# Twelve saved tiles instead of eight, and a new order of work around group 0, in a conditioned residual block

## The reference

```python
hidden = concatenate([cond, cond], -1)                      # (4, 512)
x_mean = mean(x, axis=1, keepdims=True)                     # (4, 1, 512)
fused  = concatenate([x, x_mean * ones, hidden * ones], -1) # (4, 1024, 1536)
out    = x + relu(einsum('bld,do->blo', fused, W) + b)      # W (1536, 512)
```

## Time and profile before

| | |
|---|---|
| median of 3 runs | 104.46 us |
| the profiled execution's own time | 105.41 us |
| its span, first to last instruction | 103.3 us |
| TensorE busy | 96.9 us (94%) |
| VectorE busy | 80.9 us (78%) |
| ScalarE busy | 47.3 us (46%) |
| GpSimd busy | 41.5 us (40%) |
| TensorE's granted clock | 1.0 of full speed in every slice |
| HBM traffic | 12.91 MB read, 8.39 MB written, 206 GB/s over the span |

### The profile page before, as it was taken

The page is one execution under the profiler, slowest core; times in us unless marked ns, Lnnn a source line. Parts: engine busy times, 40 slices in busy tenths (PEclk is TensorE's granted clock), DMA queues, the critical chain, the costliest instruction groups (busy, mean ns, idle before and its releaser), DMA issues.

```text
span 103.3 us, 1722 instructions
## 1 busy us (share of the span) xinstructions
PE 96.9 (94%) x523; PEld 78.2 (76%) x523; DVE 80.9 (78%) x146; ACT 47.3 (46%) x116; POOL 41.5 (40%) x37
## 2 busy tenths in 40 slices
PE   5959999999999999999999999999999999999940
PEld 2339999778888786888888886888888868888930
DVE  3173578999899999999999966999999976557630
ACT  3267335795508379497396002973951007310000
POOL 1029700000000003999846501488485089992000
PEclk9999999999999999999999999999999999999999
DMA  2999999999999997999999595000780870595994
GB/s 61 293 300 261 234 233 238 268 274 249 268 296 232 251 226 222 254 244 274 303 331 293 154 229 162 0 0 0 181 226 0 210 196 1 171 290 132 251 309 168
DMA packets 35439, 21.39 MB, mean 207 GB/s; under 512 B 2021, under 2 KB 33129, under 8 KB 35433
## 3 DMA queue, kind: packets, MB, share of 16 engines
q1 hardware_dynamic: 33848, 20.13, 78.9%
q10 hardware_dynamic: 1584, 1.18, 4.3%
HBM read 12.91 MB, written 8.39 MB: 206 GB/s over the span
## 4 chain that ended last, share of the span: by engine, by line
PE 89%; ACTq 4%; ACT 2%; issue 0%; DVE 0%
PE ps_y L459 76%; PE ps_y L560 4%; PE ps_y L562 4%; PE ps_y L561 4%; ACTq L168 2%; ACTq L158 2%; PE ps_mean L478 1%; PE ps_const L527 1%; ACT xh L259 1%; ACT w1h L252 1%; ACT L244 0%; DVE w L449 0%; PE ps_y L583 0%; ACT act_warm L244 0%
## 5 line engine op out<-in xcount | busy, mean ns | idle before, releaser
L234 POOL TENSOR_TENSOR xa<-xa,back 128x512 f32 x28 | 36.1, 1314 | 45.1 <-DVE back L346 45.1
L459 PE MATMUL ps_y<-xh,w1h 128*128 (+2 forms) x128 | 43.9, 370 | 1.1 <-ACT w1h L252 1.1
L459 PE MATMUL ps_y<-xl,w1h 128*128 (+2 forms) x128 | 43.0, 363 | 0.0
L459 PE MATMUL ps_y<-xh,w1l 128*128 (+2 forms) x128 | 42.9, 363 | 0.0
L259 ACT ACTIVATE xh<-ps_xt 128x512 fp32r<-128x512 f32 (+1 forms) x36 | 19.8, 550 | 19.4 <-DVE ps_xt L333 19.4
L459 PEld LDWEIGHTS ps_y<-xh,w1h 128*128 128x128 f32 x128 | 22.6, 188 | 6.7 <-ACT xh L259 1.6
L339 DVE TENSOR_TENSOR xl<-ps_xt,xh 128x512 fp32r<-128x512 f32 (+1 forms) x36 | 22.2, 618 | 4.7 <-ACT xh L259 4.7
L333 DVE STREAM_TRANSPOSE ps_xt<-xa 128x512 f32<-128x512 f32 (+1 forms) x36 | 22.3, 642 | 4.5 <-DMA xa<-in_x_dram 4.2
L459 PEld LDWEIGHTS ps_y<-xh,w1l 128*128 128x128 f32 x128 | 22.6, 189 | 3.8
L459 PEld LDWEIGHTS ps_y<-xl,w1h 128*128 128x128 f32 x128 | 22.7, 189 | 3.5
L277 ACT ACTIVATE relu_t<-ps_y,bias 128x512 f32<-128x512 f32 x20 | 13.5, 686 | 16.7 <-DVE bias L380 15.3
(11 more groups left out here) (34 smaller groups left out, 34.1 us busy)
## 6 DMA issues: line engine op xcount, KB each, us to landing
xa<-in_x_dram SPq DMA_DIRECT2D x60, 128.0 KB, 4.3
out_dram<-xa SPq DMA_DIRECT2D x28, 256.0 KB, 4.1
w<-in_L_cond_W_dram SPq DMA_DIRECT2D x4, 256.0 KB, 6.2
w<-in_L_cond_W_dram SPq DMA_DIRECT2D x2, 512.0 KB, 6.9
w<-in_x_dram SPq DMA_DIRECT2D x4, 256.0 KB, 3.9
out_dram<-w SPq DMA_DIRECT2D x3, 256.0 KB, 3.3
xa<-in_x_dram ACTq DMA_DIRECT2D x4, 128.0 KB, 4.2
w<-in_L_cond_W_dram SPq DMA_DIRECT2D x4, 64.0 KB, 3.2
```

What stands on the lines that cost most here:

```text
L234: nc.gpsimd.tensor_tensor(rows, rows, back[:, t], ALU.add).then_inc(added, 1)
L459: return nc.tensor.matmul(ps_y[:, t, ls], lhs, rhs, start=start, stop=stop, skip_group_check=True)
```

## The change

On the loads: block 0 and 1 of W1 are loaded as before by SP and ScalarE's queue. Then both load the second half of group 0's x, and W1's blocks 2 and 3 follow, all by SP (before they were shared, and came ahead of that half). x of group 1 goes ahead of the condition vector.

In group 0: TensorE multiplies blocks k = 0 and 1 by halves of x (256 columns), and blocks 2 and 3 by all 512 columns. The high part of W1's block 0 is made half by ScalarE, half by VectorE (`DVE_T`).

In group 1: tiles 0 and 1 are computed together, k by k, then tiles 2 and 3 one at a time.

On the way out: 12 tiles are saved instead of 8 (`SAVED = 3 * NK`). `place(n)` says where a tile lies: tiles 0 to 3 in W1's own space (after `w1l` is made), the others in the ring of 8. A bank's freeing is counted by one semaphore, `y_free`: by the save for tiles 0 to 11, by relu from tile 12 on. So tile (4, 0) starts after relu(12).

In the bias: `mean_terms(1)` stands ahead of the constant row and of `sum_bias(0)`. `w2x` has two buffers, and the batches' sums alternate between two PSUM banks. `const_product` and `mean_bias(0)` move from tile (2, 1) to tile (2, 2), and `mean_bias(b)` for b = 1, 2, 3 moves into the fourth tile of its group, behind the products of k = 0, where before it stood in front of that tile.

In the loops: VectorE carries pieces of x in steps n = 2 to 17 (`X_TURNS`; before 4 to 19) and ScalarE behind relu(n) for n = 6 to 13 and 16 to 23 (`X_ROUNDS`; before 8 to 23).

```diff
-    SAVED = H * NK
-
-    def steps_of_x(n, ahead):
-
-        return 1 if SLOTS <= n // NK + ahead < G else 0
+    SAVED = 3 * NK
+
+    X_TURNS = range(2, 2 + NK * (G - SLOTS))
+    X_ROUNDS = (*range(6, 6 + 2 * NK), *range(4 * NK, 6 * NK))
...
+    DVE_T = NK // 2
...
+        def place(n):
+
+            return w1[:, n] if n < NK else relu_t[:, (n - NK) % RELU_RING]
...
+        def mean_bank(b):
+
+            return (ps_mean, ps_const)[b % 2]
...  (SP)
-            load_w1(sp, 2, NK, LOW)
             load_x0(sp, 1, LOW)
+            load_w1(sp, 2, NK, ORDER)
+            load_x(sp, 1, ORDER)
             sp.wait_ge(cond_zeroed, 1)
...
-            load_x(sp, 1, ORDER)
             load_x(sp, 2, ORDER)
...  (ScalarE)
-            load_w1(act, 2, NK, HIGH)
             load_x0(act, 1, HIGH)
...
+                ts = slice(0, NK if k else DVE_T)
+                nc.scalar.activation(as_tiles(w1h[:, k])[:, ts], by_tile(w1[:, k])[:, ts], ACT.Copy).then_inc(w1h_ready, 1)
...
             def save(n):
                 act.wait_ge(y_ready, n + 1)
-                nc.scalar.activation(relu_t[:, n % RELU_RING], ps_y[:, n % Y_BANKS], ACT.Copy).then_inc(y_saved, 1)
+                if n < NK:
+                    act.wait_ge(w1l_ready, n + 1)
+                nc.scalar.activation(place(n), ps_y[:, n % Y_BANKS], ACT.Copy).then_inc(y_free, 1)
...
             for n in range(len(tiles)):
+                if n == NK:
+                    save(2 * NK + 3)
                 relu(n)
-                for _n in range(steps_of_x(n, 2)):
+                if n in X_ROUNDS:
                     x_high(n_x)
                     n_x += 1
...  (VectorE)
+            mean_terms(1)
             dve.wait_ge(const_summed, 1)
...
             sum_bias(0)
-            mean_terms(1)
+            sum_bias(1)
             n_x = pieces_to(SLOTS)
             for n in range(len(tiles)):
-                if n == 2:
-                    sum_bias(1)
-                elif n == NK * (H + 1):
+                if n == X_TURNS[2 * NK]:
                     sum_bias(2)
-                elif n == NK * H * (B - 1):
-                    sum_bias(B - 1)
+                elif n == X_TURNS[-1] + 5:
+                    sum_bias(3)
                 turn_back(n)
-                for _n in range(steps_of_x(n, 3)):
-                    if n % NK == 0:
+                if n in X_TURNS:
...
+                    if n_x == pieces_to(SLOTS + H):
+                        mean_terms(2)
+                    elif n_x == pieces_to(SLOTS + 2 * H):
+                        mean_terms(3)
...  (TensorE)
+            pe.wait_ge(y_free, 2)
+            for k in range(NK):
+                pe.wait_ge(xl_ready, pieces_to(1) + k + 1)
+                for t in (0, 1):
+                    last = product(1, k, t)
...
+            for g in range(H + 1, LAST):
+                for t in range(NK):
+                    pe.wait_ge(y_free, NK * (g - 1) + t + 1)
+                    for k in range(NK):
+                        if t == 0:
+                            pe.wait_ge(xl_ready, pieces_to(g) + k + 1)
+                        elif g % H == 0 and t == 3 and k == 1:
+                            mean_bias(g // H)
+                        last = product(g % SLOTS, k, t)
+                    last.then_inc(y_ready, 1)
```

More of the change, by code:

```diff
@@ L276, in relu @@
                     act.wait_ge(bias_ready, g // H + 1)
-                nc.scalar.activation(relu_t[:, slot], products, ACT.Relu,
-                                     bias=bias[:, g // H, t, g // H:g // H + 1]).then_inc(relu_done, 1)
+                nc.scalar.activation(place(n), products, ACT.Relu,
+                                     bias=bias[:, g // H, t, g // H:g // H + 1]).then_inc(relu_done if n < SAVED else y_free, 1)
             x_high(0)
+            w1_high(0)
             x_high(1)
-            w1_high(0)
             w1_high(1)
-            for k in range(2, NK):
-                x_high(k)
-                w1_high(k)
-            for n in range(NK, pieces_to(H) - 2):
+            for n in range(2, NK + 2):
                 x_high(n)
-            save(0)
-            x_high(pieces_to(H) - 2)
-            x_high(pieces_to(H) - 1)
-            for n in range(1, NK):
-                save(n)
+            w1_high(2)
+            x_high(NK + 2)
+            w1_high(3)
+            x_high(NK + 3)
+            n_x = pieces_to(1)
+            for k in range(NK):
+                x_high(n_x + k)
+                save(k)
             n_x = pieces_to(H)
@@ L342, in turn_back @@
             def turn_back(n):
[L343 removed]
+                if n < SAVED:
+                    dve.wait_ge(relu_done, n + 1)
+                else:
+                    dve.wait_ge(y_free, n + 1)
                 if n >= BACK_RING:
                     dve.wait_ge(added, n + 1 - BACK_RING)
[L346 removed]
+                nc.vector.transpose(back[:, n % BACK_RING], place(n).rearrange("p (lb om) -> p lb om", om=Q)
                                     ).then_inc(turned_back, 1)
@@ L495, in _ @@
                         pe.wait_ge(w1h_ready, k + 1)
-                    if half == 1 and k == NK - 1:
-                        pe.wait_ge(xl_ready, NK * H)
-                        for t in range(NK):
-                            mm(t, ls, w1h[:, k, t], xh[:, 0, k, ls])
-                            mm(t, ls, w1h[:, k, t], xl[:, 0, k, ls])
-                            mm(t, ls, w1l[:, k, t], xh[:, 0, k, ls], stop=True).then_inc(y_ready, 1)
-                        break
-                    for t in range(NK):
-                        mm(t, ls, w1h[:, k, t], xh[:, 0, k, ls], start=(half == 0 and k == 0))
@@ L506, in _ @@
-                    pe.wait_ge(xl_ready, NK * half + k + 1)
-                    for t in range(NK):
-                        mm(t, ls, w1h[:, k, t], xl[:, 0, k, ls])
-                    if half == 0 and k > 0:
-                        group0_low(half, k - 1)
-                    elif half == 1:
-                        group0_low(half, k)
-                if half == 0:
-                    group0_low(half, NK - 1)
-            for t in range(NK):
-                pe.wait_ge(y_saved, t + 1)
+                    group0(k, ls, w1h, xh, start=(half == 0 and k == 0))
@@ new lines, in _ @@
+                    pe.wait_ge(xl_ready, NK * half + k + 1)
+                    group0(k, ls, w1h, xl)
+                    if half == 1:
+                        group0(k, ls, w1l, xh)
+                if half == 0:
+                    for k in range(NK // 2):
+                        pe.wait_ge(w1l_ready, k + 1)
+                        group0(k, ls, w1l, xh)
+            for k in range(NK // 2, NK):
+                pe.wait_ge(w1h_ready, k + 1)
+                pe.wait_ge(xl_ready, NK + k + 1)
+                if k < NK - 1:
+                    group0(k, slice(0, NL), w1h, xh)
+                    group0(k, slice(0, NL), w1h, xl)
+                    pe.wait_ge(w1l_ready, k + 1)
+                    group0(k, slice(0, NL), w1l, xh)
+                else:
+                    pe.wait_ge(w1l_ready, k + 1)
+                    for t in range(NK):
+                        product(0, k, t).then_inc(y_ready, 1)
```

105 lines of the change are left out of this document (57 added, 48 removed).

## The result

The changed kernel takes 110.25 us (109.71 to 110.84, 4 runs) against 104.54 us (104.31 to 104.93, 4 runs) for the kernel before, measured beside it: a ratio of 1.054 [1.047, 1.061]. It is slower, as forecast, but by 5.7 us and not by 3.85. The time lies 0.55 us above the upper end of the range. The profiled execution took 110.84 us, with a span of 109.0 us, so 5.7 us more than the span of before. Both profiled executions are slower than the median of their kernel, by 0.6 us here and by 0.95 us before.

The account below looks back on a forecast made before the run. TensorE's products bound the kernel, with the store path 0.2 us shorter; the changed store path decides, its span 107.15 - 103.3 = +3.85 us, so 104.46 + 3.85 = 108.3 us, range 106.4 to 109.7 (8 in 10).

Parts of the forecast that it names:

- a wait for relu(12): At group 4's start TensorE wants bank 0 at 53.4 and gets it at 55.1, a new wait of about 1.6 us.
- ten adds behind `mean_terms(3)`: GpSimd's last run holds ten adds, not eight, from 84.55 to 97.55, 4.0 us later than 93.52.
- the last term of the tail: From GpSimd's last add at 97.55 to the span's end: 9.8 - 0.2 us, giving 107.15.
- Behind the last add: Store queue after GpSimd's last add: 9.8 - 0.2 us, nothing added for group 5's stores draining (at most 1 us).
- C: Rival: batch 3's bias write lands only at 95.5 and delays group 5's stores; 110.6 us at worst, 109.5 at half; chance 0.11.
- Start of GpSimd's run: GpSimd's last run of adds starts at 84.55 instead of 82.96, as VectorE's second half is 1.6 us late.
- TensorE's wait for the second half of x: In group 0, TensorE can use that half at about 10.45, 0.35 us after it asks.
- The adds: GpSimd's last run: ten adds of 1.3 us, the median duration, 13.0 us in all.
- the wait near 7.5 for W1's block 1: Group 0: TensorE finishes eight halves by 7.46, waits 0.7 us for block 1's copy, goes on at 8.2.
- group 2 did not start earlier: Forecast had group 1 end and group 2 start at 29.8, from a shorter group 0 and waits removed by pairs.
- Rival A: TensorE's path stays the longest, GpSimd's last add by 93.5 and bank 0 on time: faster, 103.9 us; chance 0.11.
- Port: VectorE instructions with two SBUF inputs slow GpSimd's adds: 0.5 us more on one or two adds, none if last_rows come at 97.

Follow-up runs that it names:

- e2: Changed kernel with batch 3's bias write and read put ahead of group 4's stores in SP's queue; 109.91 us, 1.049 of the kernel before.
- e3: Changed kernel with relu(12) ahead of two of ScalarE's pieces of x; 108.94 us, 1.040 of the kernel before.
- e5: Kernel before with only VectorE's pieces of x two steps earlier (2 to 17), with their mean_terms and bias sums; 107.88 us, 1.033 of the kernel before.
- e7: Kernel before with group 1's tiles 0 and 1 as a pair and ScalarE's saves moved between its pieces; 104.62 us, 1.003 of the kernel before.
- e9: Kernel before with the change's start (loads, W1 order, block 0 copied by two engines) and group 1's pair; 104.48 us, 1.001 of the kernel before.
- e6: Changed kernel with VectorE's pieces from step 4, relu(12) early, and the old loads, W1 copy and group 0 order; 106.36 us, 1.021 of the kernel before.
- e10: Kernel before with mean_terms(3) moved behind the turns back of tiles 20 and 21; 104.48 us, 1.003 of the kernel before.
- e11: Changed kernel with mean_terms(3) moved behind the turns back of tiles 18, 19 and 20; 109.54 us, 1.048 of the kernel before.
- e8: Changed kernel with VectorE's pieces from step 4, relu(12) early, and batch 0's bias ahead of mean_terms(1); 107.90 us, 1.032 of the kernel before.

## Why the prediction was wrong

The direction and the two mechanisms (a wait for relu(12), ten adds behind `mean_terms(3)`) held; the time was 0.55 us outside the range. The step that failed is the last term of the tail: "97.55 + 9.8 - 0.2 = 107.15", with "group 5's stores drain just ahead of group 6's, for which I add nothing (at most 1 us)".

- *Behind the last add.* I had 9.6 us; the profile has 11.1, which is 1.5 us. The 9.8 us of before belong to a queue in which group 5's four stores were issued by 91.31, 2.2 us before the last add ended, and 2.1 MB moved behind that add (9.78 us at 215 GB/s). In the new order the bias line's write and read hold back group 5's stores until 94.69. Their fourth is issued at 98.06, when the last add is already done, and 2.8 MB move behind it (11.09 us at 250 GB/s). Group 6's four stores, behind a queue that is still full, take 4.2 us to issue (98.10 to 102.31) instead of 3.0 (93.54 to 96.54), with the last group's rows behind them. I had seen this queue and made of it a rival (C, 0.11; 109.5 to 110.6, which holds the measured time). C began with a write that lands at 95.5 and gave 109.5 at half the delay. The write landed at 94.3 (91.98 + 2.30) and group 5's stores began at 94.69, about half way from the forecast's 93.6 to C's 96, and so the result is nearer to C than to my forecast. e2 takes the hold away and the term returns to 10.0; e3 and e5 show it at 11.1 to 11.2 with other starts. How much of it is the stores and how much the last rows, which wait for the same bias, e2 does not separate. For the stores speaks that SP issues them without a gap, and that VectorE's last instruction ends at 103.41, before the last stores are issued.
- *Start of GpSimd's run.* 85.38 instead of 84.55, so 0.8 us. TensorE's wait for the second half of x was 1.04 us and not 0.35 (the last of its four transfers took 5.85 us to land), so group 2 started near 30.4, and the save of tile 11 came at 43.45 and not at 42.65. All that follows is 0.8 us late. I had also missed that the save of tile 10 holds relu(0) until 40.64, but that is not on the path: ScalarE idles 0.26 us ahead of tile 11's save. The landing differs from one execution to the next. In the seven profiled kernels with this start and twelve saves TensorE took up the second half of x between 10.15 and 10.98, and after has the latest. In e2, where it was 10.16, relu(0) started at 39.82 (40.64) and the run of adds at 84.60 (85.38): the same 0.8 us all along the chain. This part of the miss is in good part chance.
- *The adds.* Ten took 12.53 us, not 13.0: -0.45 us. I had multiplied the median duration, but adds in a row follow one another every 1.25 us. The rows of before say so: 10.56 us for eight with a last one of 1.81 leaves 8.75 for seven. Together 1.5 + 0.8 - 0.45 = 1.85 us, which is 5.7 - 3.85.

What held: the first product at 6.54 (6.5), batch 0's bias at 40.1 (39.85), relu(12) at 54.98 (54.2), one wait of TensorE for it of 1.4 us (1.6), ten adds in the last run, the bias write at 90.96 (90.4), stores as the last stretch. e3 agrees with the wait's price: 1.4%, about 1.5 us, with intervals that leave 0.3 to 2.5%. e5 confirms that of the turns alone.

What did not: the wait near 7.5 for W1's block 1 was not there. Its copy ran from 7.02, not 7.43, and TensorE took it up at 7.80 instead of 8.2. And group 2 did not start earlier. I had 29.8 by a shorter group 0 and waits that the pair removes. The second half of x gave the gain back at once (chain: 10.98, then 126 products without a break, and the constant at 37.29). One reading of before was incomplete: beside the 0.2 us SP also waited 2.0 us for VectorE's L372. Of these waits only the 0.2 us leave a gap between issues, so the sum does not change. e7 and e9 show that in the kernel before the pair and the start are worth nothing either (1.003, 1.001). e6 shows the start is worth 0.012 beside twelve saves and late turns: the same edit has two prices, because in e6 something waits for it (the bank at the start of group 1).

I also had Rival A (faster) at 0.11, resting on "TensorE's path stays the longest". It did not: TensorE is idle for the last 5 us of after.

**Port.** I had named that VectorE's instructions with two inputs in SBUF slow GpSimd's adds, and left it out of the sum, rightly for this kernel: its last rows start at 97.64, when the adds end. e2, e10 and e11 show what happens otherwise. In e2 the eighth to tenth adds and VectorE's instructions take turns:

| start us | us | engine | instruction | ends |
|---|---|---|---|---|
| 93.35 | 1.29 | GpSimd | add 8 | 94.64 |
| 93.58 | 1.61 | VectorE | L394 | 95.19 |
| 94.60 | 1.75 | GpSimd | add 9 | 96.35 |
| 95.83 | 1.07 | VectorE | L394 | 96.90 |
| 96.30 | 1.75 | GpSimd | add 10 | 98.05 |
| 96.93 | 1.40 | VectorE | L475 | 98.33 |

Each ends behind the one above it, by a little less than it takes alone: L394 by 0.55 us (0.69 alone), an add by 1.15 (1.25), L475 by 0.28 (0.42). The Trainium skill, SBUF — State Buffer, section "SBUF: two separate sides", says that the ports shared by the two engines are locked for a whole instruction and the other engine blocks meanwhile. The excesses measured agree with that: 1.61 - 0.69 = 0.92, 1.07 - 0.69 = 0.38, 1.40 - 0.42 = 0.98 and, in e10, 1.47 - 0.49 = 0.98 us on VectorE, each less than one add (1.25 us). They follow from how much of the add was still to run: L394 loses 0.92 us where 1.06 us of the add were left, and 0.38 where 0.52 were. A split of bandwidth would rather have slowed both L394 alike.

## What to carry to other kernels

A stretch "from the last X to the end" read from a trace is not a constant that can be moved: it holds only while what is already in the queue at X stays the same, so count the bytes and the small ordered transfers still to go, and divide by the bandwidth of the last full stretch. When a loop's pieces move earlier, count what now stands behind the last long instruction block; here two steps of a loop cost 3% with the matrix engine's program untouched (e5). And before an instruction is taken out of its place because it looks like a delay (e8), ask what it was covering.
